# A decoder block on one core: 64-wide matmuls put in both column halves, and three instruction queues in a new order

## The reference, cut to what matters

```python
def delta_rule(q, k, v, beta, decay):        # B=4, H=16, T=512, DK=DV=128
    def step(S, inp):
        qt, kt, vt, bt, gt = inp
        Sd = S * gt[..., None]
        v_pred = einsum('bhk,bhkv->bhv', kt, Sd)
        S_new = Sd + einsum('bhk,bhv->bhkv', kt * bt[..., None], vt - v_pred)
        return S_new, einsum('bhk,bhkv->bhv', qt, S_new)
...
o = lam * delta_rule(.., beta_fast, decay_fast) + (1 - lam) * delta_rule(.., beta_slow, decay_slow)
o = o / rms(o) * onorm_w * sigmoid(x @ g1_w @ g2_w + g2_b);   x = layernorm(x + o @ wo)
```

## Time and profile before

| what | us |
|---|---|
| median of 3 runs (4428.7 to 4443.83) | 4435.1 |
| the profiled execution | 4440.9 |
| its span, first to last instruction | 4439.1 |
| attention stage, about | 0 to 2916 |
| state-space stage, about | 2916 to 3665 |
| expert stage, about | 3665 to 4439 |
| PE busy over the span | 4124.4 (93%) |
| DVE busy | 3216.0 (72%) |
| ACT busy | 2271.0 (51%) |
| POOL busy | 882.2 (20%) |

### The profile page before, as it was taken

How to read it: one execution, slowest core, us unless ns; L and a number is a source line. 1 busy time by engine, 2 the same in 40 slices (tenths; PEclk the granted TensorE clock), 3 DMA queues, 4 the chain that set the end, 5 groups by cost and what they waited for, 6 DMA issues and landing times. The chain is left out here.

```text
span 4439.1 us, 180073 instructions
## 1 busy us (share of the span) xinstructions
PE 4124.4 (93%) x76786; PEld 2578.2 (58%) x76786; DVE 3216.0 (72%) x5520; ACT 2271.0 (51%) x5547; POOL 882.2 (20%) x1800
## 2 busy tenths in 40 slices
PE   7999999999999999999999999857878768999999
PEld 4676776777777767767677676623333334444443
DVE  4888888888888888888888888569999981222211
ACT  4666666666666666666666666434344331111110
POOL 1323232333323233332323233100000000000000
PEclk9999999999999999999999999878889888999999
DMA  2212221221212212121212212142333223000000
GB/s 74 68 59 64 63 66 60 62 67 56 75 52 71 64 59 73 57 69 59 69 59 66 64 59 68 38 133 68 99 85 96 76 73 142 10 19 29 0 19 10
DMA packets 133579, 277.33 MB, mean 62 GB/s; under 512 B 20860, under 2 KB 62352, under 8 KB 129328
## 3 DMA queue, kind: packets, MB, share of 16 engines
q1 hardware_dynamic: 132640, 265.61, 19.3%
q10 hardware_dynamic: 144, 0.20, 0.0%
HBM read 235.09 MB, written 30.67 MB: 60 GB/s over the span
## 5 line engine op out<-in xcount | busy, mean ns | idle before, releaser
L414 PE MATMUL a_pb<-a_x_t,a_w_qkv 128*128 128x512 f32 x1536 | 835.9, 636 | 17.2 <-DMA a_x_t<-in_x_t 8.7
L1293 DVE TENSOR_TENSOR a_nq<-a_nq,a_tot 128x512 f32<-128x512 f32 (+1 forms) x768 | 492.5, 683 | 121.7 <-PE a_pb L437 81.2
L1255 DVE SCALAR_TENSOR_TENSOR a_acc<-a_pb,a_taps,a_acc 128x511 f32<-128x511 f32 (+2 forms) x576 | 425.2, 738 | 41.9 <-ACT a_acc L848 12.9
L1985 PE MATMUL m_p_y<-m_h,m_ident 128*128 128x512 f32 x512 | 283.7, 706 | 121.5 <-DVE m_h L2183 121.5
L437 PEld LDWEIGHTS a_pb<-a_nq,a_ks 128*32 128x32 f32 x20480 | 212.4, 110 | 172.7 <-issue 145.3
L2451 PE MATMUL f_pb<-f_x_t,f_w_gu 128*128 128x512 f32 x704 | 308.0, 592 | 0.0
L414 PEld LDWEIGHTS a_pb<-a_x_t,a_w_qkv 128*128 128x128 f32 x1536 | 239.0, 190 | 99.8 <-issue 67.8
L2505 ACT ACTIVATE f_gate<-f_pb 128x512 f32<-128x512 f32 x132 | 78.8, 597 | 410.6 <-PE f_pb L2451 274.3
L2177 DVE TENSOR_TENSOR_SCAN m_h<-m_da,m_h 128x2048 f32<-128x2048 f32 x64 | 283.2, 4424 | 6.5 <-ACT m_da L2106 1.0
L1657 POOL COPY a_apt<-a_apt_fine 32x256 f32<-32x256 f32 x256 | 100.5, 393 | 907.8 <-DVE a_apt_fine L1311 882.3
L1985 PEld LDWEIGHTS m_p_y<-m_h,m_ident 128*128 128x128 f32 x512 | 112.3, 227 | 283.9 <-DVE m_h L2183 148.7
(11 more groups left out here) (295 smaller groups left out, 8973.8 us busy)
## 6 DMA issues: line engine op xcount, KB each, us to landing
a_rows<-rows SPq DMA_DIRECT2D x192, 512.0 KB, 3.8
a_amp_sums<-amp_sums SPq DMA_DIRECT2D x64, 508.0 KB, 3.7
attn_o<-a_o_t SPq DMA_DIRECT2D x64, 256.0 KB, 2.5
m_b_rows<-ssm_bc SPq DMA_DIRECT2D x64, 256.0 KB, 3.7
m_c_rows<-ssm_bc SPq DMA_DIRECT2D x64, 256.0 KB, 4.5
m_o_t<-attn_o SPq DMA_DIRECT2D x16, 1024.0 KB, 8.5
a_w_qkv<-in_w_qkv SPq DMA_DIRECT2D x48, 256.0 KB, 2.9
f_w_gu<-in_w_gu SPq DMA_DIRECT2D x3, 1536.0 KB, 18.7
```

The costliest lines, as they stand in the source:

```text
L414: mm = nc.tensor.matmul(pb[:, V_BANK if i == P_V else KQ_BANK], w_qkv[:, i, k], x_t[:, k, b * T:(b + 1) * T], start=(k == 0), stop=(k == D ...
L1255: last = nc.vector.scalar_tensor_tensor(acc[:, i, d:T], src[:, 0:T - d], taps[:, i, 3 - d:4 - d], acc[:, i, d:T], ALU.mult, ALU.add)
L1293: last = nc.vector.tensor_tensor(part, part, spread(blocks, list(part.shape)), ALU.mult)
L1985: nc.tensor.matmul(p_y[:, et], ident[:], h[:, (b * DS + n) % 3, et], start=(n == 0), stop=(n == DS - 1), skip_group_check=True).then_inc(s ...
```

## The change

Three things, in one edit.

1. Level 6 is laid out anew: the slow rate's four matmuls go to one column half of the array (and half of the PSUM partitions), the fast rate's to the other, alternating. The copies on ACT are split by rate, since source and destination partitions now differ: `copy_64` has 4 instructions of 64 partitions x 256 in place of 2 of 64 x 512, `copy_w(6)` and `copy_y64` have 2 in place of 1.
2. `slot` of PE, ACT and DVE has a new order, and its boundary lies elsewhere (`later` is s.at(-2)). POOL's `slot` is counted from another slot number, with its six steps in the same order. SP's is untouched.
3. `ssm_first` stands in slots 65 to 70; on SP its loads stay where they were.

```diff
-        wy64_psum = pb[:, INV].rearrange("p (i t) -> p i t", i=PAIRS)
-        p64_psum = pb[0:P // 2, 0:2].rearrange("p n (i k t) -> p (n i) k t", k=2, t=P // 2)
+        p64_psum = pb[:, 0].rearrange("p (c k t) -> p c k t", c=TT, k=2)
+        w64_psum = pb[:, INV, 0:TT * P // 2].rearrange("p (c t) -> p c t", c=TT)
+        y64_psum = pb[:, INV, TT * P // 2:TT * P].rearrange("p (c t) -> p c t", c=TT)
...
+        def half_of(rate):
+            return slice(rate * P // 2, (rate + 1) * P // 2)
...
+                    if level == 1:
+                        need(pe, kept_32, s.due(0, 1, 0))
                     if level == 6:
-                        pe.wait_ge(kept_32, s.due(0, 1, 1))
+                        for c in range(TT):
+                            for rate in (SLOW, FAST):
+                                mm = nc.tensor.matmul(p64_psum[half_of(rate), c], ks[:, n2, rate, c * P:c * P + P // 2],
+                                                      nq[:, n2, rate, :, c * P + P // 2:(c + 1) * P],
+                                                      start=True, stop=True, tile_position=(0, rate * P // 2))
...
-                        mm = nc.tensor.matmul(wy64_psum[P // 2:P, i], apt_64[:, i], x_half[:, i],
-                                              start=True, stop=True, tile_position=(0, P // 2))
+                    for c in range(TT):
+                        for rate in (SLOW, FAST):
+                            mm = nc.tensor.matmul(w64_psum[half_of(1 - rate), c], apt_64[:, rate * TT + c],
+                                                  x_half[:, rate * TT + c], start=True, stop=True,
+                                                  tile_position=(0, (1 - rate) * P // 2))
...
-                        mm = nc.tensor.matmul(wy64_psum[0:P // 2, i], w_64[P // 2:P, i],
-                                              y_inv[P // 2:P, s.ring(0, 2), i, P // 2:P],
-                                              start=True, stop=True, tile_position=(P // 2, 0))
+                            mm = nc.tensor.matmul(y64_psum[half_of(rate), c], w_64[P // 2:P, i],
+                                                  y_inv[P // 2:P, s.ring(0, 2), i, P // 2:P], start=True, stop=True,
+                                                  tile_position=(P // 2, rate * P // 2))
...
-                    nc.scalar.copy(apt_64[:], p64_psum[:, :, NEG_K])
-                    nc.scalar.copy(apt[0:P // 2, s.ring(0, 2), :, P // 2:P], p64_psum[:, :, QUERY]).then_inc(kept_64, 1)
+                    for rate in (SLOW, FAST):
+                        nc.scalar.copy(apt_64[:, pairs_of(rate)], p64_psum[half_of(rate), :, NEG_K])
+                    for rate in (SLOW, FAST):
+                        last = nc.scalar.copy(apt[0:P // 2, s.ring(0, 2), pairs_of(rate), P // 2:P],
+                                              p64_psum[half_of(rate), :, QUERY])
...
-                    if s.n == UNITS - 1:
-                        ssm_first(0)
+                    if s.n == UNITS + 1:
+                        ssm_first(0)
```

More of the change, by code:

```diff
@@ L122, in over_units @@
 def over_units(slot):
-    for n in range(-3, UNITS + 4):
+    for n in range(-6, UNITS + 7):
         slot(Slot(n))
@@ L718, in slot @@
                         recur_odd(late, 1)
+                    if late.has(3):
+                        project(late, 3, P_K, 0)
                     if late.has(-2):
@@ L1095, in slot @@
                 def slot(s):
+                    later = s.at(-2)
                     late = s.at(-1)
-                    if late.has(-1):
-                        copy_u(late, 0)
-                    if late.has(-1):
-                        copy_kt(late, 0)
-                    if late.has(2):
-                        silu(late, 2, P_V)
                     if s.n == 0:
@@ new lines, in slot @@
+                    if s.n == 0:
+                        keep_g(2)
+                    if late.has(2):
+                        square_v(late)
+                    if late.has(1):
+                        copy_rows(late)
+                    if late.has(-3):
+                        tanh_gate(late)
+                    if s.n == UNITS + 4:
+                        ssm_first(FIRST_EXP)
+                    if late.has(-1):
+                        copy_u(late, 1)
+                    if s.n == 0:
+                        keep_g(3)
@@ L1175, in slot @@
-                    if s.n == UNITS:
-                        ssm_first(2)
                     if late.has(1):
                         exp_tot(late)
+                    if late.has(0):
+                        copy_w(late, 4)
                     if late.has(1):
@@ L1472, in slot @@
                 def slot(s):
+                    later = s.at(-2)
                     late = s.at(-1)
+                    if late.has(0):
+                        set_diag(late)
+                    if later.has(3):
+                        convolve(later, 3, P_K)
+                    if s.n == -1:
+                        lower(1)
+                    if later.has(2):
+                        invert(later)
+                    if later.has(0):
+                        grow(later, 4)
+                    if later.has(0):
+                        decay_nq(later, 6)
+                    if later.has(1):
+                        prepare_nq(later, NEG_K)
+                    if later.has(1):
+                        first_ks(later)
+                    if later.has(1):
+                        prepare_nq(later, QUERY)
+                    if late.has(2):
+                        convolve(late, 2, P_V)
+                    if s.n == -1:
+                        sum_widths(1)
+                    if s.n == UNITS + 6:
+                        ssm_first(3)
+                    if late.has(0):
+                        decay_nq(late, 0)
+                    if late.has(0):
+                        keep(late, 0)
                     if late.has(0):
@@ L1500, in slot @@
                         keep(late, 2)
+                    if late.has(2):
+                        dot_vvh(late)
+                    if s.n == -1:
+                        entropy(1)
+                    if late.has(-3):
+                        gate_o(late)
                     if late.has(0):
@@ L1547, in slot @@
-                    if late.has(0):
-                        decay_nq(late, 6)
-                    if late.has(1):
-                        first_ks(late)
-                    if late.has(1):
-                        prepare_nq(late, QUERY)
-                    if late.has(2):
-                        invert(late)
-                    if s.has(2):
-                        convolve(s, 2, P_V)
-                    if s.n == -1:
-                        sum_widths(2)
-                    if s.n == UNITS:
-                        ssm_first(3)
```

455 lines of the change are left out of this document (217 added, 238 removed).

## The result

The changed kernel takes 4673.2 us (median of 4 runs, 4665.2 to 4698.6) against 4439.5 beside it: ratio 1.053, 95% interval 1.050 to 1.056. The forecast was 4330 with a range to 4405. It is slower, by 234 us where 110 less was expected.

A forecast was written before the change was run, and what follows sets the result against it. PE's queue was taken to bound attention at 43.3 us a period; a loop through POOL would leave 41.5, so 4440.9 - 112 + 8 for the seam = 4337, less 5.8 to the median: 4330 us, range 4250 to 4405.

The forecast's parts named there:

- PE's new order: PE's queue in attention: with shorter level 6, fewer mode switches and no idle, it alone needs 39.7 us a period.
- the seam: From attention to the state-space stage: later batch costs 8 us net, with 46 us behind the last recurrence matmul.
- five cases: Whole kernel: forecast 0.50, PE floor reached 0.20, gain turned into waits 0.13, halves not overlapping 0.09, slower 0.08.
- slower: Rival, chance 0.08: PE's `w_64` waits for POOL's `spread_y`, delaying `products0` and the period; 4499 us at a 4.5 us wait.
- Level 6 in halves: PE's level-6 groups in alternating column halves take 1.09, 0.55 and 0.55 us, together 2.0 us less a period.
- Fewer visits to the full array: PE's full-array visits between tiled groups fall from 17 to 12 a period, 0.95 us less.
- The closed loop: Longest loop, through DVE, PE and POOL, sums to 42.0 us and sets the period at 41.5.
- The wait that it forecast at `invert`: DVE's `invert` waits some 1.0 us a period for POOL's `norms_dens`, with later DVE steps queued behind it.
- ACT's extra copies hidden: Split copies, 8 instructions in place of 4, add about 0.3 us a period on ACT, hidden in its idle time.
- The rule weighed in the prediction: Skill's rule for PE: weight loads overlap matmuls in flight only across row groups, shrinking the 2.0 us to nearly nothing.

The follow-up runs named there:

- e1_halves: Kernel before, its order of work kept, with only the new level-6 halves and split copies: 4384.6 us, ratio 0.988; timed again 0.991.
- e2_order: Kernel after, its new order of all queues kept, with the old level-6 groups: 4698.5 us, ratio 1.059.
- e4_seam: Kernel after with the first state-space batch put back inside the last periods: 4654.9 us, ratio 1.049.
- e3_spread: Kernel after with five groups of PE moved so that groups of tiled matmuls hardly ever adjoin: 4675.0 us, ratio 1.053.
- e6_half: Kernel after with half the matmuls of products 2, products 4, w_fine 1 and x_fine 1 left out from unit 4 on: 4479.3 us, ratio 1.010.
- e8_x1: e1_halves with project P_Q 3 moved ahead of products 1 and x_fine 1 ahead of recur_even 1 on PE: 4393 us, ratio 0.991.
- e7_apart: e1_halves with ten groups of PE's queue moved one to three places so tiled groups stand further apart: 4476.8 us, ratio 1.009.
- e5_cluster: Kernel before with w_fine 1, products 2 and x_fine 1 placed side by side on PE: 4575.4 us, ratio 1.032.

## Why the prediction was wrong

The step that failed is the sum of PE's new order, "PE's queue alone would need 43.3 - 2.0 - 0.95 - 0.63 = 39.7 us". It took the time of a queue for the sum of its groups' times, in whatever order they stand. The groups do sum to nearly that: with each at its duration in a period without stalls they make 40.2 us in after (39.8 with each at its median at full clock). What the sum leaves out is that instructions must arrive. The account of a period of after: 40.2, plus 3.4 of stalls at block boundaries, plus 1.8 of the same work at a lower granted clock (PE's busy time is 42.0), plus 1.1 of data waits, is 46.5; measured 46.56. The 1.8 is what is left of the busy time over the 40.2; the granted clock of 0.96 alone, 4% of 46.56, says 1.9. Against the forecast of 41.5 that is 5.06 us in each of some 62 periods, 314 us of the miss of 343; the seam adds 7. Of the 22 left, 12 are the distances of the two profiled executions to their medians (the forecast took 5.8 off, and after's execution lies 6.5 below its median), and 5 lie ahead of the first `gate_logits` (236.1 us in after, 231.5 in before).

The rows of before held the sign. PE idled 26.9 us in listed waits there, and 19.4 of it was "issue", nearly all in the middle of tiled groups, up to 1.5 us at a time. The longest rows, and one such stall in the very period of the earlier trace rows:

```profile
PE a_pb L461 <- issue: 8.1, 10, 1.2
PE a_pb L485 <- DVE a_state L1351: 7.3, 13, 0.7
PE a_pb L472 <- issue: 3.7, 5, 1.0
PE a_pb L437 <- issue: 3.2, 4, 1.5
```

```profile
1530.57 0.65 PE L437 MATMUL a_pb<-a_nq,a_ks 128*32 128x32 f32 x50
1532.35 0.33 PE L437 MATMUL a_pb<-a_nq,a_ks 128*32 128x32 f32 x14 [1.14 <-issue]
```

I read idle of 0.63 a period as small and didn't ask what it was made of. None of the five cases had the mechanism, and the chance of slower, 0.08, stood on another one: `w_64` does wait for `spread_y`, in 37 of 46 periods, but for 0.47 us a period, not the 3.6 from which it would decide.

Point by point:
- Level 6 in halves: right for `products 6` (1.09, as forecast), a little short for the other two (0.68 each, not 0.55). L441, L575 and L586, to be held against 1.96, 1.11 and 1.14 in the earlier trace rows:

```profile
1515.03 1.09 PE L441 MATMUL a_pb<-a_nq,a_ks 128*64 128x128 f32 x16
1524.11 0.68 PE L575 MATMUL a_pb<-a_x_half,a_apt 64*64 64x64 f32 x16 [0.46 <-POOL a_y_inv L1700]
1528.75 0.68 PE L586 MATMUL a_pb<-a_y_inv,a_w 64*64 64x64 f32 x16
```

  These end-to-end times are 1.76 less together; I gave 2.0. In e1_halves it was 1.63 of PE's work.
- Fewer visits to the full array: about right, 0.95 forecast. With each group at its median duration at full clock a period sums to 42.5 us in before and 41.5 in e2_order, which has the new order alone, and to 40.75 in e1_halves and 39.8 in after: the order takes some 1.0 off the sum in either pair. The stalls and the clock more than ate it.
- The closed loop: its terms can't be seen while the stalls cover them. The wait that it forecast at `invert`, 1.0 us, is there with 0.46:

```profile
DVE a_invs L1441 <- POOL a_dens L1670: 21.0, 46, 0.8
```

- ACT's extra copies hidden: e1_halves, which has them all, gained; no row of it shows a wait for them. They cost more than was put: 8 of 0.36 us in place of 4 of 0.58, 0.6 us a period where the estimate was 0.3.
- The seam: nearly right. No DMA wait stands ahead of the first projection, and what follows the last recurrence matmul is the chain foreseen. PE's timeline there, its rounds mostly at the lower clock (0.57 granted from 3096 to 3140):

```profile
3089.43 1.06 PE L533 MATMUL a_pb<-a_nq,a_state 128*128 128x128 f32 x4
...
3100.37 3.78 PE L667 MATMUL a_pb<-a_x_t 128*128 128x512 f32 x4 [4.92 <-DVE a_x_t L1458]
3107.36 3.78 PE L667 MATMUL a_pb<-a_x_t 128*128 128x512 f32 x4 [3.21 <-DVE a_x_t L1458]
3114.35 5.94 PE L674 MATMUL a_pb<-a_x_t,a_w_qkv 128*48 128x512 f32 x8 [3.21 <-DVE a_x_t L1458]
...
3130.28 2.07 PE L683 MATMUL a_pb<-a_w_qkv 16*128 16x512 f32 x2 [1.35 <-ACT a_x_t L1093]
```

  It runs from 3090.5 to the next stage's first DVE instruction at 3140.5, 50 us; 46 were forecast. By e4_seam the late batch costs 15 us net (34 more behind, 19 less ahead), where the sum had 8.

What stays open: what starts a block's transfer. The sum with "about 50 instructions in, 2.9 us" comes within 0.6 us of every row (e3_spread and e6_half with the waits off the boundary taken off), but it is a fit: in after the transfers start a median 1.2 us after PE has begun a block, in before 1.1, but anywhere from 0.2 to 4.3 (5th to 95th percentile, after). What holds the period of e1_halves and its two variants at 42.5 is not shown: each change there only moved the idle time, which a ring of engines near 42.5 would do too. And whether the new order without stalls would beat e1_halves: the two kernels that removed stalls from it also changed data waits or left out work.

## What to carry to other kernels

A queue of many small matmuls has a second bound beside its busy time: how fast instructions arrive. Here a block of 256 (128 matmuls with their loads) came at best every 3.3 us, and was used up in 1.3 us of tiled work, so keep long full-array matmuls between groups of tiled ones; and when an order is changed, sum instructions over each stretch, not only times. A stall named "issue" in the middle of a group is this sign, and worth a count modulo 256 even when it is small. Moving a group for spacing can cost as much in data waits; try each move by itself. The best kernel here is e1_halves, the old order with the new level-6 groups (e8_x1 equals it): 0.9 to 1.2% faster than before.

## What the runs showed of the hardware that I had not expected

- The stalls named "issue" inside groups lie 256 instructions or a multiple of that apart (to one), and most end 2.2 to 2.8 us after the start of the latest instruction transfer. The closest that two transfers start is 3.2 to 3.4 us, in every kernel here.
- Such a stall is paid again in the clock. In the even part of after PE stood still 45 times for 1.5 to 3.4 us, and within 3 us behind 35 of these the granted clock is at its lower level, 0.50; over the stretch it is 0.96. In e7_apart it idles 2.7 us a period, in 224 pieces of which none is over 1.5 us, and the granted clock is 0.99. Length alone does not sort them: in e3_spread only 14 are that long, and the clock is 0.98. In e5_cluster 1.07 us of added stalls a period came with 1.10 us of slower work, at 0.97.
- Alternating column halves run side by side, loads included, at 64 as at 32 columns: level 6's 16 matmuls take 1.09 us where they took 1.96. In the trace the two matmuls of a pair start 6 to 7 ns apart and a pair every 109 ns, the distance of single ones in before. The rule weighed in the prediction (the Trainium skill, TensorE: Matmul & The Clock Gate, Part 3: Packing small matmuls) doesn't hold here.
